# Expert weight loads of a fused attention and mixture-of-experts kernel, issued from ScalarE's queue in place of SyncE's

## The reference

```
x = x + xattn0(layernorm(x), k, skip, ctx)         # a causal convolution of v*ctx along 256 values, 8 by 8 heads
x = x + ffn0(layernorm(x), W, A, B, router)        # low-rank experts, top 2 of 16
x = x + xattn1(layernorm(x), ctx, wq, wkv, wp)     # 16-head cross attention, projections in fake int8
x = x + ffn1(layernorm(x), router_w, gate_w, up_w, down_w, shared)

def ffn1(flat):                                    # 2048 tokens of 256
    scores = sqrt(softplus(flat @ router_w.T))
    idx = top_k(scores + expert_bias, 4)           # 4 of 32 experts for each token
    probs = normalised scores[idx]
    out = sum over experts e of probs[:, e] * clamped_swiglu(flat, gate_w[e], up_w[e], down_w[e])
    return out + clamped_swiglu(flat, shared weights)
```

## Time and profile before

| | before |
|---|---|
| median of 3 runs | 722.79 us (722.42 to 728.71) |
| the profiled execution | 728.71 us, of which 726.9 us span and 1.8 us around it |
| busy share of the span | PE 80%, DVE 66%, ACT 52%, POOL 51% |
| the chain that ended last | PE 39%, SP's queue 31%, DMA 12%, DVE 9% of the span |
| weights (`arena<-in_w`) | 8 transfers of 1536 KB |

### The profile page before, as it was taken

How to read it: one execution, slowest core, us unless ns; L and a number is a source line. 1 busy time by engine, 2 the same in 40 slices (tenths; PEclk the granted TensorE clock), 3 DMA queues, 4 the chain that set the end, 5 groups by cost and what they waited for, 6 DMA issues and landing times.

```text
span 726.9 us, 14275 instructions
## 1 busy us (share of the span) xinstructions
PE 579.1 (80%) x4045; PEld 467.2 (64%) x4045; DVE 482.2 (66%) x1462; ACT 379.5 (52%) x1107; POOL 373.7 (51%) x526
## 2 busy tenths in 40 slices
PE   1588899999969966986998779973069999999920
PEld 1487788777758855775786556652058878888810
DVE  1646657777897753789657796677437776555587
ACT  1002456666765542782757765673036666666610
POOL 6757847564472536874316521054715555555550
PEclk9999999999988986997999989996569999999975
DMA  8989999999999964321004990269535555555688
GB/s 279 218 214 334 335 334 332 334 325 317 317 317 328 307 206 139 119 67 52 30 17 145 334 330 29 74 187 343 178 110 159 162 158 157 158 161 161 208 278 277
DMA packets 135740, 155.02 MB, mean 213 GB/s; under 512 B 15248, under 2 KB 124944, under 8 KB 135408
## 3 DMA queue, kind: packets, MB, share of 16 engines
q1 hardware_dynamic: 117536, 122.50, 56.8%
q0 software_dynamic: 7632, 20.98, 8.0%
q10 hardware_dynamic: 10496, 10.62, 4.6%
HBM read 53.92 MB, written 100.28 MB: 212 GB/s over the span
## 4 chain that ended last, share of the span: by engine, by line
PE 39%; SPq 31%; DMA 12%; DVE 9%; issue 4%; ACT 2%; POOL 2%; ACTq 0%; DVEq 0%; POOLq 0%
SPq L1350 28%; PE ps L605 11%; PE pS L578 6%; PE pc L557 3%; DMA stage<-in_pad 3%; DMA expert_rows<-stage 3%; DMA work<-y_rows 2%; SPq L1333 2%; PE pS L537 2%; DMA expert_rows<-stage,ixl 2%; PE ps L478 2%; PE ps L348 2%; PE ps L523 1%; PE po L597 1%; DVE xs L1048 1%
## 5 line engine op out<-in xcount | busy, mean ns | idle before, releaser
L1323 POOL DMA_INDIRECT y_rows<-tk,work x95 | 94.1, 990 | 81.8 <-ACT tk L1231 74.9
L557 PE MATMUL pc<-arena,tk 128*128 128x128 f32 x768 | 109.2, 295 | 15.8 <-DVE arena L773 8.5
L557 PEld LDWEIGHTS pc<-arena,tk 128*128 128x128 f32 x768 | 97.4, 203 | 28.7 <-DVE arena L773 15.0
L1299 POOL TENSOR_TENSOR arena<-arena 128x512 f32<-128x512 f32 x64 | 90.4, 1430 | 19.8 <-ACT arena L1099 19.5
L605 PE MATMUL ps<-arena,work 128*128 x380 | 99.8, 386 | 0.3 <-ACT work L1226 0.3
L985 DVE TENSOR_SCALAR work<-ps 128x256 f32<-128x256 f32 x95 | 40.2, 423 | 67.9 <-PE ps L605 67.3
L1313 POOL DMA_INDIRECT expert_rows<-stage,ixl x64 | 63.7, 995 | 35.6 <-DMA stage<-xn_rows 17.9
L1164 ACT ACTIVATE work<-pS,work 128x128 f32<-128x128 f32 x256 | 72.5, 370 | 3.7 <-DVE work L791 3.7
L605 PEld LDWEIGHTS ps<-arena,work 128*128 128x128 f32 x380 | 66.0, 194 | 5.9 <-issue 0.7
L578 PE MATMUL pS<-arena,tk 128*128 x190 | 59.6, 395 | 2.2 <-ACT tk L1221 2.1
L791 DVE TENSOR_REDUCE work<-pS 128x4 f32<-128x512 f32 x64 | 43.8, 685 | 26.3 <-PE pS L537 26.2
(11 more groups left out here) (271 smaller groups left out, 1369.0 us busy)
## 6 DMA issues: line engine op xcount, KB each, us to landing
expert_rows<-stage SPq DMA_DIRECT2D x32, 2080.0 KB, 21.7
work<-expert_rows SPq DMA_DIRECT2D x95, 130.0 KB, 2.2
arena<-in_w SPq DMA_DIRECT2D x8, 1536.0 KB, 14.7
stage<-xn_rows SPq DMA_DIRECT2D x64, 130.0 KB, 2.4
xn_rows<-xnD ACTq DMA_DIRECT2D x16, 512.0 KB, 7.5
work<-y_rows SPq DMA_DIRECT2D x16, 512.0 KB, 5.2
tk<-in_tk SPq DMA_DIRECT2D x1, 2048.0 KB, 9.3
out<-xs SPq DMA_DIRECT2D x16, 128.0 KB, 3.2
```

The lines of the kernel that those rows point to most:

```text
L557: i = pe.matmul(pv, tk[:, h, 128 * d:128 * d + 128], kvv[:, ci, :, :].rearrange("p b (i h j) -> p (b i) h j", i=8, h=8)[:, :, hl, :], star ...
L1299: pool.tensor_tensor(kv[kk % 4][:, c, half, :].rearrange("p (i h j) -> p i h j", h=8, i=8), i0, i1, ALU.mult).then_inc(s_kv, 1)
L1323: pool.indirect_dma_start(out=Yr, out_offset=bass.IndirectOffsetOnAxis(ap=xg[n % NX][:, 256:257].bitcast(U32), axis=0), in_=y[n % 4], in_o ...
```

## The change

The issues of `w0` and `w1` move from SP's program to ACT's, with the same waits, the same transfers and the same semaphore. On ACT they stand at ticks 2771 and 3233, where SP had them at 2620 and 3130. Nothing else is different; the lines of ACT's program behind the insertion move down by 5 or 9.

```diff
-            "oT": 1137, "xnA": 212, "xnB": 747, "xnD": 1190, "xd": 1196, "shw": 2459, "xr": 2571,
-            "xnC": 878, "q": 923, "PT": 1035}
+            "oT": 1137, "xnA": 212, "xnB": 747, "xnD": 1190, "xd": 1196, "w0": 2771, "shw": 2459, "xr": 2571,
+            "w1": 3233, "xnC": 878, "q": 923, "PT": 1035}
...
-        T_SP = {"fill": 1162, "st": 1855, "w0": 2620, "w1": 3130}
+        T_SP = {"fill": 1162, "st": 1855}
...
+                for _ in at(t, T_ACT["w0"], 1, 1):
+                    act.wait_ge(s_uT, 2 * NP)
+                    act.wait_ge(s_swb, 1)
+                    for e0 in range(0, early, 4):
+                        act.dma_start(wv_[:, e0:e0 + 4, :], a_w[e0:e0 + 4].rearrange("e p n -> p e n")).then_inc(d_w, 16)
...
+                for _ in at(t, T_ACT["w1"], 1, 1):
+                    act.wait_ge(s_S, 4 * NB)
+                    for e0 in range(early, NE, 4):
+                        act.dma_start(wv_[:, e0:e0 + 4, :], a_w[e0:e0 + 4].rearrange("e p n -> p e n")).then_inc(d_w, 16)
...
-                for _ in at(t, T_SP["w0"], 1, 1):
-                    sp.wait_ge(s_uT, 2 * NP)
-                    sp.wait_ge(s_swb, 1)
-                    for e0 in range(0, early, 4):
-                        sp.dma_start(wv_[:, e0:e0 + 4, :], a_w[e0:e0 + 4].rearrange("e p n -> p e n")).then_inc(d_w, 16)
-                for _ in at(t, T_SP["w1"], 1, 1):
-                    sp.wait_ge(s_S, 4 * NB)
-                    for e0 in range(early, NE, 4):
-                        sp.dma_start(wv_[:, e0:e0 + 4, :], a_w[e0:e0 + 4].rearrange("e p n -> p e n")).then_inc(d_w, 16)
```

## The result

| | before | changed kernel |
|---|---|---|
| median | 722.79 us | 733.99 us (733.08 to 736.29, 5 runs) |
| ratio | | 1.0153 (95% interval 1.0125 to 1.0182) |
| profiled execution | 728.71 us, span 726.9 us | span 733.0 us |

The change costs 11.2 us, slower by 1.5%. The forecast was 724.7 us with a range of 719 to 732; the result is above it. Two comparisons on other occasions gave 1.0136 and 1.0155.

The account below looks back on a forecast made before the run. From 252 to 495 us PE, ACT and DVE bound it, then a scatter and stage-load ladder to 532 us, then PE. Terms +2.7 (w0) and -0.8 (w1) gave +1.9 us on 722.8, so 724.7 us, range 719 to 732.

Parts of the forecast that it names:

- The old place of w0 on SP: SP near 402 us: removing the five issues, which hold SP for 9.63 us, gains 0 us.
- The new place of w0: ACT after 435.87 us: five issues take 7.6 us, delaying the chain by +2.7 us, between 0 and +4.7 us.
- The delay is then 7.6 - 4.9 = +2.7 us: ACT at w0's new place: the 7.6 us taken by five issues, less 4.9 us free, gives the delay.
- the 4.9 us of slack: ACT from 435.87 us: it must resume by 440.7 us for PE to get qT in time, leaving 4.9 us free.
- the second rival: PE at 443 to 448 us: ACT held 9.6 us, PE's clock stays low, +3.7 us; sum +7.6 us, 730.4 us; chance 0.18.
- xr behind w0 in ACT's queue: xr load issued at 448.13 us, queued behind w0's transfers: 0 us taken, +1.5 us kept as an end.
- w1 leaves the ladder's start: POOL's last 23 scatters from 495.11 us: without any stall they end at 522.9 instead of 527.21 us, at most 4.3 us gained.
- w1 in the ladder's middle: POOL's scatters, about 507 to 524 us: w1's flow causes one 3.5 us stall; ends are none or two.
- I take one stall: Scatters under late w1: one full seven-scatter round meets the transfer, so -4.3 + 3.5 = -0.8 us.
- The third rival: POOL's ladder of scatters and stage loads: two stalls under late w1, total +5.4 us, 728.2 us; chance 0.15.
- w1 hidden from PE's start by 5 us or more: PE's first expert matmul at about 533 us: w1 lands near 524 to 528 us, so it stays hidden.
- The two unlikely cases: The second rival (ACT hold and low PE clock, chance 0.18) and the third rival (two ladder stalls, chance 0.15).

Follow-up runs that it names:

- hold_4: Kernel before with six 128x512 copies added on ACT at tick 2771, about 4 us of hold, no transfer moved: ratio 1.0026, +1.9 us.
- hold_8: Kernel before with twelve 128x512 copies added on ACT at tick 2771, about 8 us of hold, no transfer moved: ratio 1.0110, +8.1 us.
- w0_alone_b: Against the kernel before, only w0's issues moved to ACT, w1 left on SP, second measurement: ratio 1.0115, +8.3 us.
- whole_b: The changed kernel measured again beside its two halves, against the kernel before: ratio 1.0155, +11.2 us.
- after: Profiled execution of the changed kernel, w0 and w1 both on ACT: span 733.0 us; median 733.99 us, ratio 1.0153 against the kernel before.
- after_again: The changed kernel measured once more, on a third chip, against the kernel before: ratio 1.0136, +9.8 us.

## Why the prediction was wrong

The sign of the sum was right, and so was where to look. But each of the two terms left something out, and both were far too small; the second came out with the other sign.

**The old place of w0 on SP, 0 us.** Right: from SP's first stage load to PE's L388 it is 163.4 us before and 163.4 us after, so SP's freedom near 402 us gained nothing.

**The new place of w0, +2.7 us; it was +5.7 us in the trace.** The length of the hold was nearly right: 8.32 us (7.5 to 8.2 us in the other traces) against 7.6 us, inside the bounds. The step that failed is "The delay is then 7.6 - 4.9 = +2.7 us", which has two faults.

First, what PE does after the gap was counted at full speed, a term put at nothing. In the trace of the changed kernel the 4.9 us of slack held: 8.32 - 3.35 = 4.97 us. PE's L523 then came 3.5 us late, and PE ran at half speed: L523 lost 0.3 us, and from L537 to the copy from `po` it was 4.79 against 2.70 us, another 2.1 us. That makes 5.9 us at that point, of which 5.7 us reached the statistics. This mechanism stood in the second rival, with a price of 3.7 us, and was set aside because one gap is less than the idle time before the clock's first fall. It came with a gap of 3.35 us.

Second, the 4.9 us were read from an execution in which PE was late by its own low clock. Where PE is at full clock, 2.9 to 3.1 us are free (hold_4, hold_8, w0_alone_b, whole_b). This fault does not show in the trace of `after`, but it does in `whole_b`, the same kernel, with a gap of 4.78 us.

**xr behind w0 in ACT's queue, 0 us.** Right: no wait for it appears.

**w1 leaves the ladder's start, -4.3 us.** Right in what it described: the first stop is gone, 13 scatters pass without one. But only 3.3 us of the 4.3 us are that stop; 0.8 us are the 17th scatter's, which came when `w1` had long landed. And the first stop is not a fixed price: it is 0.9 to 4.7 us in the eight traces with `w1` at its old place.

**w1 in the ladder's middle, one stall of 3.5 us; it was 10 us.** This is the step with the larger error, "I take one stall". 37.8 us for the ladder less the 27.8 us of 22 steps at 1.264 us leave 10.0 us, where two stalls of 3.5 us were the upper end. Two things were wrong. The round was taken as "seven scatters on" everywhere, and the 17th scatter's is four: 13.7 us passed in it, where POOL would have the buffer back after 5.1. And the price of a stall was read where `w1` was ending. Before, `w1` began 8 us ahead of the first of the 23 scatters and slowed a scatter (7.26 us to land), but it was all but over when the first of their buffers were reloaded. In the changed kernel the stage loads issued from 509.8 to 516.3 us took 5.8 to 9.5 us, where the 22 loads of before from 480 to 521 us took 2.1 to 3.6 us. Each of the two groups of stops cost about 5 us. The third rival (two stalls, +2.7 us) had the right count and was 3 us short.

**w1 hidden from PE's start by 5 us or more.** Right: the third transfer was issued at 510.15 us and landed 20.6 us later, 530.8 us, with PE's first tile at 541.21 us. It landed later than the 524 to 528 us forecast, but everything behind it was later too.

**The chances.** The two unlikely cases, each given under 0.2, came together. They do not exclude each other, and the range should have held their sum: 7.6 + 2.7 + 0.8 = +11.1 us. That this is so near the measured +11.2 us is luck: the second rival's parts are 8.4 us, where 5.7 us were found in the trace, and the third's ladder is +2.7 us, where it was +5.7 us.

The rule that issuing from several engines saves only a usually small issue time (the Trainium skill, "DMA: Bandwidth & Descriptors", "Issuing engines are not separate DMA queues") would have given 0 for the first term. The trace says 8.32 us for five issues at once, and 0.37 to 0.74 us each when spread.

## What to carry to other kernels

Five transfers of 1536 KB issued one behind another held the issuing engine until about the time when the first had landed; three took 1.5 us. On an engine that computes, spread such issues, or leave them on SP. Slack on a path is only as good as the execution that it was read in: look whether the engine that grants it was itself slow there. When a buffer ring is priced, find for each use the use before it in the program's order: where two sequences alternate, a round can be four steps and not seven. Price a background transfer from loads that ran beside it from end to end, not beside its tail. Parts of `w1` at two or three places cost nothing here where the whole in the ring's middle cost 5 to 8 us, though none of them beat the old place.

## What was not expected of the hardware

Five transfers of 1536 KB take 8.32 us to issue in a row and 0.37 to 0.38 us each when 4 to 9 us lie between them (0.74 us after a distance of 2.5 us). PE's granted clock went to its lower level after a gap of only 3.35 us (3.11 us in `after_again`), for some 6 us; it had been there once some 7 us earlier. Work put into that gap kept the clock up at that place in both traces. Between 475 and 490 us the granted clock is 1.00 in some executions and 0.89 in others, also of one and the same kernel, and no run here shows why.
